# First feed-forward of a two-layer kernel: the last six weight chunks rounded on VectorE instead of GpSimd, and two row blocks issued at other places

## The reference, cut to what matters

```python
def _quantized_matmul(x, w, scale):
    wq = w.astype(jnp.float8_e4m3fn).astype(x.dtype)     # weights rounded to 8 bits, computed in f32
    return jnp.einsum('bsi,io->bso', x, wq) * scale
gate = jax.nn.silu(_quantized_matmul(x, gate_w, gate_scale))   # 256 -> 768
up = _quantized_matmul(x, up_w, up_scale)                      # 256 -> 768
return _quantized_matmul(gate * up, down_w, down_scale)        # 768 -> 256
...
x = x + _L0_xattn_ref(_layernorm(x), ctx_1024, ...)
x = x + _L0_ffn_ref(_layernorm(x), ...)
x = x + _L1_xattn_ref(_layernorm(x), ctx_1024, ...)
x = x + _L1_ffn_ref(_layernorm(x), ...)
```

## Time and profile before

| | us |
|---|---|
| median of 3 runs | 722.06 (721.88 to 723.37) |
| profiled execution | 722.73 |
| its span in the trace | 720.9 |
| busy: TensorE / VectorE / ScalarE / GpSimd | 660.1 / 548.9 / 479.7 / 436.0 |

### The profile page before, as it was taken

The page is one execution under the profiler, slowest core; times in us unless marked ns, Lnnn a source line. Parts: engine busy times, 40 slices in busy tenths (PEclk is TensorE's granted clock), DMA queues, the critical chain, the costliest instruction groups (busy, mean ns, idle before and its releaser), DMA issues.

```text
span 720.9 us, 16231 instructions
## 1 busy us (share of the span) xinstructions
PE 660.1 (92%) x5782; PEld 527.8 (73%) x5782; DVE 548.9 (76%) x1180; ACT 479.7 (67%) x982; POOL 436.0 (60%) x618
## 2 busy tenths in 40 slices
PE   2789999988899999999999999999999999999784
PEld 1567777667788877888888888888888888876442
DVE  3699999999787877676777676676767766766887
ACT  1577877756466576666666666666666666658994
POOL 2378878878877545565656656665656554464500
PEclk9999999999999999999999999999999999999997
DMA  8200003203201000000000100000100000000001
GB/s 282 77 9 9 10 9 117 70 1 106 86 1 38 15 1 2 15 30 9 23 24 17 28 9 25 23 16 16 31 9 16 15 1 3 1 1 1 31 29 60
DMA packets 26019, 22.83 MB, mean 32 GB/s; under 512 B 5041, under 2 KB 24402, under 8 KB 25810
## 3 DMA queue, kind: packets, MB, share of 16 engines
q1 hardware_dynamic: 24160, 20.92, 9.2%
q10 hardware_dynamic: 1778, 0.86, 0.4%
HBM read 19.67 MB, written 2.10 MB: 30 GB/s over the span
## 4 chain that ended last, share of the span: by engine, by line
POOL 38%; issue 26%; PE 15%; DVE 14%; ACT 3%; ACTq 1%; POOLq 1%; DVEq 0%
POOL rstd L734 14%; POOL pr L702 5%; POOL p_n L709 5%; PE banks L1594 2%; POOL w L725 2%; POOL w_raw L722 2%; PE banks L1613 2%; PE banks L1614 2%; DVE h_sum L1093 2%; DVE hid_b L1086 2%; POOL var L732 1%; POOL qk_norm L644 1%; DVE h_magic_b L1091 1%; DVE half L852 1%; POOL hid_lo L671 1%
## 5 line engine op out<-in xcount | busy, mean ns | idle before, releaser
L734 POOL TENSOR_TENSOR rstd<-var,minus_half 128x8 f32<-128x8 f32 x64 | 106.1, 1657 | 5.0
L709 POOL TENSOR_TENSOR p_n<-pr,pinv 128x256 f32<-128x256 f32 x64 | 39.3, 614 | 75.7 <-DVE pinv L1001 75.7
L702 POOL TENSOR_TENSOR pr<-pr,rstd 128x256 f32<-128x256 f32 x63 | 38.6, 613 | 74.1 <-DVE pr L1011 74.0
L1316 ACT ACTIVATE kT<-banks,gk_q 128x512 f32<-128x512 f32 x64 | 44.0, 688 | 49.1 <-PE banks L1755 49.1
L1745 PE MATMUL banks<-m_hi,z_hi 128*128 128x256 f32 x256 | 74.9, 293 | 0.7 <-DVE z_lo L992 0.6
L1745 PE MATMUL banks<-m_hi,z_lo 128*128 128x256 f32 x256 | 72.3, 283 | 0.0
L1745 PE MATMUL banks<-m_lo,z_hi 128*128 128x256 f32 x256 | 72.3, 282 | 0.0
L992 DVE TENSOR_TENSOR z_lo<-banks,z_hi 128x512 fp32r<-128x512 f32 x64 | 43.9, 686 | 29.1 <-ACT z_hi L1301 29.0
L1039 DVE TENSOR_REDUCE sums<-q_sq 128x4 f32<-128x512 f32 x64 | 43.7, 683 | 25.2 <-ACT q_sq L1340 25.2
L1362 ACT ACTIVATE qT<-banks 128x512 f32<-128x512 f32 x64 | 38.2, 597 | 32.9 <-PE banks L1849 32.9
L1007 DVE TENSOR_REDUCE pmax<-banks 128x4 f32<-128x256 f32 x64 | 27.0, 422 | 41.1 <-PE banks L1776 41.0
(11 more groups left out here) (194 smaller groups left out, 2059.2 us busy)
## 6 DMA issues: line engine op xcount, KB each, us to landing
w_raw<-in_L_xattn_Wq SPq DMA_DIRECT2D x4, 512.0 KB, 5.8
wo_raw<-in_L_xattn_Wo SPq DMA_DIRECT2D x1, 2048.0 KB, 9.2
k_ctx<-in_ctx SPq DMA_DIRECT2D x16, 128.0 KB, 2.7
w_raw<-in_L_ffn_w_gating SPq DMA_DIRECT2D x16, 128.0 KB, 2.3
out_x<-x_sb SPq DMA_DIRECT2D x4, 512.0 KB, 2.9
x_sb<-in_x SPq DMA_DIRECT2D x1, 1536.0 KB, 9.3
a_ctx<-in_ctx SPq DMA_DIRECT2D x16, 64.0 KB, 1.8
w_raw<-in_L_xattn_Wk SPq DMA_DIRECT2D x2, 512.0 KB, 9.1
```

The costliest lines, as they stand in the source:

```text
L702: pool.tensor_tensor(pr[:, u % 2, :, :], pr[:, u % 2, :, :], roots_of[:, HC:2 * HC].unsqueeze(2).to_broadcast([P, HC, S]), ALU.mult).then_ ...
L709: pool.tensor_tensor(p_n[:, u % 2, :, :], pr[:, u % 2, :, :], pinv[:, u % 2, :].unsqueeze(2).to_broadcast([P, HC, S]), ALU.mult).then_inc( ...
L734: pool.tensor_tensor(rstd1[:, par, :], var1[:, :], minus_half[:, :].to_broadcast([P, 2 * HC]), ALU.pow).then_inc(root1, 1)
L1316: act.activation(kT[u % 2][:, :, :].rearrange("p h n -> p (h n)"), bank[2][:, :], ACT.Copy, scale=gk_q[:, :]).then_inc(kT_ready, 1)
```

## The change

The chunks 12 to 17 are rounded wholly on VectorE, by a new helper `w0_rounded_here` that issues the masks and then the add and the subtraction. Their twelve GpSimd instructions (an add and a subtraction for each of six chunks) are gone from GpSimd. `W0_LATE` goes from 13 to 12. Chunks 12 and 13 now stand on VectorE ahead of `rows_updated(15)`, 14 to 17 in units 3 to 6. On VectorE `hidden(1)` goes ahead of the four `normal`, and `rows_updated(15)` behind `hidden(2)` and chunk 13, with `rows_updated(14)` ahead of chunk 12. On GpSimd the last `weights_lo(23)` goes behind `hidden_lo(23)`.

```diff
-W0_LATE = W0_CHUNKS - 5
+W0_LATE = W0_CHUNKS - 6
...
+        def w0_rounded_here(dve, n):
+
+            w0_magic(dve, n)
+            dve.wait_ge(magic_steps, 2 * n + 2)
+            dve.wait_ge(w0_steps, 2 * n)
+            dve.tensor_tensor(w0_raw[:, w0_part(n)], w0_raw[:, w0_part(n)], rnd[:, n % 2, :], ALU.add).then_inc(w0_steps, 1)
+            dve.wait_ge(w0_steps, 2 * n + 1)
+            dve.tensor_tensor(w0[:, w0_part(n)], w0_raw[:, w0_part(n)], rnd[:, n % 2, :], ALU.subtract).then_inc(w0_steps, 1)
...
             w0_rounded(pool, 11)
             probabilities0(NT - 1)
-            w0_rounded(pool, 12)
             rows_biased(NT - 1)
             hidden_lo(0)
             weights_lo(0)
             hidden_lo(1)
-            w0_rounded(pool, W0_LATE)
             weights_lo(1)
...
-                weights_lo(u)
+                if u < NG * J0 - 1:
+                    weights_lo(u)
                 hidden_lo(u)
-                if u <= W0_CHUNKS - W0_LATE:
-                    w0_rounded(pool, W0_LATE + u - 1)
             run_groups(J0, step, 2)
+            weights_lo(NG * J0 - 1)
...
             w0_magic(dve, 11)
-            w0_magic(dve, 12)
             exponential_sums0(NT - 1)
             hidden(0)
+            hidden(1)
             for r in range(GT, 2 * GT):
                 normal(r, f_xhat, f_xhat_ready, fT_done)
-            hidden(1)
-            w0_magic(dve, W0_LATE)
             rows_updated(NT - 2)
+            w0_rounded_here(dve, W0_LATE)
+            hidden(2)
+            w0_rounded_here(dve, W0_LATE + 1)
+            rows_updated(NT - 1)
 
             def step(g, j, par):
                 u = J0 * g + j
                 hidden(u)
-                if u == 2:
-                    rows_updated(NT - 1)
...
                 if u <= W0_CHUNKS - W0_LATE:
-                    w0_magic(dve, W0_LATE + u - 1)
+                    w0_rounded_here(dve, W0_LATE + u - 1)
...
-            run_groups(J0, step, 2)
+            run_groups(J0, step, 3)
```

## The result

The changed kernel takes 725.35 us (median of 8 runs, 724.26 to 727.95) against 722.37 for the kernel before (8 runs beside them, 721.37 to 723.55). The ratio is 1.0042 with an interval of 1.0025 to 1.0059: slower by 3.0 us (1.8 to 4.3 by the interval), where 1.65 was forecast. The range of the forecast ended at 725.2, 0.15 under the measured median. The profiled execution is 726.14 with a span of 724.3, against 722.73 and 720.9. Two disturbed executions further down, of 919 and 2160 us, stand outside every comparison.

The account below looks back on a forecast made before the run. GpSimd was taken to bound the stretch from 173 to 192 us. VectorE's delays of +2.3 us less 0.65 for the last w_lo gave +1.65 on 722.06, so 723.7 us, range 720.9 to 725.2.

Parts of the forecast that it names:

- What bounds the kernel: From 173 to 192 us GpSimd at 3.5 us a turn bounds, not TensorE at 2.86 a unit; at most 3.5 to win.
- Step 1: At down(0): VectorE's chunks 12 and 13 delay the row add of tile 15, so down(0) starts at 176.2, 2.3 us late.
- Step 2: Units 2 to 5: everything moves by 2.3 us, most is won back, chunk 17 delays down(5) to 193.1; both steps cost 2.3.
- How the two engines hold each other: A VectorE mask, normal or SBUF add meeting a GpSimd tensor operation waits for its end, then takes 0.15 or about 0.28.
- the race for chunk 17: Ahead of down(5): hid_lo(6) starts 0.2 us before chunk 17's subtraction and holds it; cost 2.3 us, or 1.4 if subtraction leads.
- the price that I gave for that rule: If the port rule held for chunk 15's add and subtraction, 0.7 us more at down(5): sum +2.4, or 724.4.
- Step 3: End of the feed-forward: with the last w_lo behind it, hid_lo(23) starts earlier; 0.65 us gained, between 0 and 0.7.
- The real gain: Second rival: VectorE is hardly held, down(5) at 190.05; -1.4 us with the last w_lo's gain, 720.7; chance 0.13.
- the adds that slip through: First rival: VectorE's adds and subtractions slip between GpSimd operations, down(5) at 191.4, 722.0 us; chance 0.33 with its neighbour.
- The worse case: Third rival: VectorE's adds hold GpSimd in turn, delaying hid_lo of units 4 to 6; +4.3 - 0.65, 725.7; chance 0.07.
- Its sign: Third rival, unit 5: it decides from the point at which hid_lo(5) starts before chunk 16 is added.
- The chances: Whole kernel: slower 0.50, the same 0.38, faster 0.12; the likeliest case, VectorE held, 0.47.

Follow-up runs that it names:

- both gaps filled: The changed kernel with 11 extra unread products on TensorE ahead of down(0) and 8 ahead of down(5): 723.82 us, ratio 1.0014.
- w_lo was away: The changed kernel with GpSimd's w_lo of units 1 to 6 put off to units 7 to 12, two a unit: 726.26 us, ratio 1.0052.
- the first experiment: The kernel before with only the last w_lo moved behind the last hid_lo: 722.35 us, ratio 0.9996.
- come at the next gap: The changed kernel with 11 extra unread products on TensorE ahead of down(0) only: 725.54 us, ratio 1.0050.
- made by a gap alone: The kernel before with five extra row-moment instructions on VectorE ahead of rows_updated(15): 727.20 us, ratio 1.0047.
- The last experiment: The changed kernel with 11 and 8 extra products ahead of down(0) and down(5), the last w_lo back ahead of the last hid_lo: 726.07 us, ratio 1.0044.
- rows_updated(15) first: The changed kernel with rows_updated(15) ahead of chunk 13 instead of behind it: 725.19 us, ratio 1.0033.
- two chunks: The kernel before with chunks 15 and 16 alone rounded on VectorE and the last w_lo behind the last hid_lo: 721.48 us, ratio 0.9987.
- the w_lo later: The kernel before with w_lo of units 3 to 6 put off to units 7 to 10, last w_lo behind the last hid_lo: 720.95 us, ratio 0.9974.
- one chunk: The kernel before with w_lo of units 3 to 6 put off, last w_lo moved, and chunk 15 alone rounded on VectorE: 720.81 us, ratio 0.9973.

## Why the prediction was wrong

The direction was right and the mechanism of VectorE stood as described. The sum had no term for TensorE's clock. In the profile that term is 1.0 us of the +3.4, and the median left the range by only 0.15.

- **What bounds the kernel.** Right: TensorE ran in 2.86 us per unit wherever it was not stopped, and is at that from down(6) on after the change (197.43 - 194.56 = 2.87). The three experiments that shortened GpSimd's turn took 0.5, 1.5 and 2.5 us off down(5).
- **Step 1**, down(0) at 176.2, 2.3 late: it came at 176.28 with 2.83 us idle, 2.32 late. Its inside was less exact than its end. The add of chunk 12 ran free (171.17 to 171.60, where I had it held until 172.8) and the subtraction was held instead, until 173.03 and not 173.65; the first mask of chunk 13 then took 0.84 and not 0.28. That the two misses cancel is luck. The race is a close one: in the six other profiles with chunk 12 on VectorE the add was the one held, as I had it.
- **Step 2**, down(2) to down(5) at 181.3, 184.3, 188.0 and 193.1: they came at 182.32, 185.73, 189.23 and 194.56, late by 1.0, 1.4, 1.2 and 1.5. Most of the first 1.0 is the missing clock: the two downs took 4.12 us in place of 2.78, and down(2) is at 9.91 behind outputs0(15), against 9.31 with both gaps filled. **This is the step that failed.** It moved everything behind down(0) "by these 2.3 us" at the duration that TensorE's products had before, though they now stood behind a gap of nearly 3 us, at a granted clock of 0.50. Of the 1.34 lost in the two downs, 0.99 is left at down(5). With both gaps filled the loss at down(5) is 2.72, so VectorE's part was mis-sized by 0.4 and the clock is the other 1.0.
- **How the two engines hold each other.** Right in the main: mean 495 and 745 ns against 410 free, the longest 1.40. Hid_lo(6) did win the race for chunk 17, with the cost of a whole hid_lo, and did so again when w_lo was away. The masks had run free beside the power, and so did these. Here are the add and the subtraction of chunk 15, and GpSimd's power of the last rows beside them:

```profile
184.70 0.43 DVE L430 TENSOR_TENSOR w_raw<-w_raw,rnd 128x256 f32<-128x256 f32 x1
185.16 0.42 DVE L432 TENSOR_TENSOR w<-w_raw,rnd 128x256 fp32r<-128x256 f32 x1
```

```profile
184.47 1.07 POOL L486 TENSOR_TENSOR row_rstd<-row_v,minus_half 128x4 f32<-128x4 f32 x1
```

  The first ran wholly inside 1.07 us of a GpSimd tensor operation, and the second began in it, and neither was held. The Trainium skill, "SBUF — State Buffer", section "Who interferes with whom", has the pair of ports held for the whole instruction. Most rows here agree (a subtraction ended 0.28 behind the hid_lo that it met); this pair does not, and the price that I gave for that rule, 0.7, was rightly left out of the sum. Held until 185.54, the add would have ended at about 185.8, 0.28 behind as the others did, and not at 185.13.
- **Step 3**, -0.65: -0.68 in the profile of the changed kernel, and 0.72 when taken back. The nine profiles named with the first experiment put it at 0.67 to 0.75. Not seen in the medians by itself.
- **The rivals.** The real gain and the adds that slip through are refuted by 2.83 and 3.2 us of stops on VectorE. The worse case named 725.7 for another reason, GpSimd held in turn. That is not what happened. Its sign was hid_lo(5) ahead of the add of chunk 16, and that add had ended at 188.62, before hid_lo(5) began at 189.17. Hid_lo(6) started by its own release from ScalarE, and the largest stretch of a hid_lo here is 1.46 against 1.30. It lay near the result by chance.
- **The chances.** 0.45 and the 0.07 of the worse case add up to 0.52 for slower and not 0.50, a slip without weight.
- **The whole.** In the profile the account closes. Against the forecast down(5) is 1.5 late: 0.4 of VectorE's part, 1.0 of the clock, and 0.1 from ahead of outputs0(15). In the medians it is less sure. The four runs of the changed kernel with a mean clock of 0.987 to 0.989 took 724.26 to 724.56. The 52 runs of the kernel before with 0.986 or more have a median of 722.43, so that is 2.1 more, and from the rows VectorE's part is 2.72 - 0.68 = 2.0. The other four, at 0.982 to 0.985, lie 1.6 to 3.5 higher. So I read the median of +3.0 as 2.0 of VectorE's and about 1 of the clock's. The first is shown by the rows and by both gaps filled. Of the second the size at down(5) is shown by profiles (0.99), and that gaps bring such falls is supported by three experiments with one profile each: taken away, come at the next gap, and made by a gap alone. The gap of 3.04 without a fall stands beside them. The share of the clock behind these gaps in the median is only argued. The last experiment, with both gaps filled too, came out at 726.07, and the difference between a short and a long fall at the opening moves a run by 1.3 to 2.7 us. A mean clock of 0.985 or less was seen in 15 of the 43 runs of the six kernels with a gap of 2 us or more here, and in 25 of 121 runs of six without: more often, but not clearly so. What decides in which run the clock falls stays open, and so does why two experiments (rows_updated(15) first, and the last w_lo at its old place) came out about 1.5 us slower than their profiles of this stretch.

## What to carry to other kernels

When a change makes a gap on TensorE of 2 us or more in a stretch where it was busy, price the work behind the gap at the longer durations as well, as a case that may or may not come: here down(0), the four transposes behind it and the first products of down(1) took 1.3 us more, on a change whose own cost was 2. And before moving work from GpSimd to VectorE, ask what on GpSimd could simply be later: putting off four w_lo gained 1.6 us, where moving six chunks lost 3.0 (both with the last w_lo moved). A count shared by two engines makes them wait for each other's turn even where the data does not.

## What the runs showed of the hardware

- In the profiles of this stretch TensorE stood still for 2 us or more in eight places between busy stretches. Its granted clock fell to 0.50 behind five of them (2.83, 2.50, 2.09, 2.62 and 2.96 us) and stayed at 1.00 behind three (3.04, 2.29 and 2.29). In the six profiles without such a gap (before, both gaps filled with either place of the last w_lo, two chunks, the w_lo later, one chunk) it did not fall here at all. So a long gap did not always bring it, and elsewhere in the trace it fell behind shorter ones: in the kernel before at 152 to 157 us, behind a stretch in which TensorE was busy for 0.65 of 2 us and no gap was longer than 1.18.
- The clock at the opening (24 to 42 us) fell too, in eleven of twelve profiles and not alike: for 3 to 4 us in nine, for over 10 in two. The first output product of the first attention came at 43.32 to 44.50 and at 45.81 to 46.05, and at 42.58 where the clock did not fall.
- In the kernel before the spread goes with the mean clock too: of its 67 runs beside the experiments (one more, of 2160 us, set aside) the 15 with a mean clock of 0.984 or 0.985 took 723.62 to 725.84, and the other 52 took 721.39 to 724.36, all but two of them 723.54 or less.
- With one gap removed the fall came at the next one, in one profile: with 11 products in the first, the clock was 1.00 at 176 to 180 us and 0.50 at 194 to 196.
- A VectorE add or subtraction with both operands in SBUF takes 0.42 to 0.43 alone, 1.37 to 1.45 when it is issued 0.11 to 0.37 us behind the start of a hid_lo of 1.26 to 1.47 us on GpSimd, 0.83 to 0.87 when it meets a w_lo of 0.74 to 0.80 so (it ends 0.27 to 0.29 behind either in all these cases), and 0.42 to 0.43 beside a GpSimd power of 1.07 us on 128x4.
